# A gated-linear-attention layer with a routed expert layer on 8 cores: rows normalised earlier, four widths of tail products, rows loaded by a transposing DMA

## The reference

```
scores = (q * exp(A)) @ (k * exp(-A)).T, lower triangle       # A = cumsum(log f) in the chunk
o      = scores @ v + (q * exp(A)) @ S
S      = exp(A_last) * S + (k * exp(A_last - A)).T @ v        # k = 1 - exp(log f)
```

## Time and profile before

| | |
|---|---|
| median of three runs | 2378.13 us |
| profiled execution: its time / span of the slowest core (core 4) | 2381.81 us / 2380.2 us |
| spans of the eight cores | 2348.0 to 2380.2 us |
| TensorE matmuls busy | 2251.3 us (95%) |
| VectorE / ScalarE / POOL busy | 1066.1 (45%) / 700.0 (29%) / 331.9 us (14%) |
| TensorE's mean granted clock, core 4 | 0.979 |
| chain that ended last: TensorE / DMA / VectorE | 71% / 14% / 8% |
| HBM read and written | 577.84 MB and 109.05 MB |

### The profile page before, as it was taken

The page is one execution under the profiler, slowest core; times in us unless marked ns, Lnnn a source line. Parts: engine busy times, 40 slices in busy tenths (PEclk is TensorE's granted clock), DMA queues, the critical chain, the costliest instruction groups (busy, mean ns, idle before and its releaser), DMA issues.

```text
span 2380.2 us, 44339 instructions; the slowest of 8 cores (2348.0 to 2380.2 us)
## 1 busy us (share of the span) xinstructions
PE 2251.3 (95%) x15680; PEld 1401.6 (59%) x15680; DVE 1066.1 (45%) x2174; ACT 700.0 (29%) x1346; POOL 331.9 (14%) x539
## 2 busy tenths in 40 slices
PE   5999998989998999999999999999999999998997
PEld 4666554556645655566444457767666586683443
DVE  6666665666655766565541231121121212211366
ACT  4444542355515553344321101121111212111000
POOL 1110110112101210111111011111101011011230
PEclk9999999999999999999999999999999999998998
DMA  7999976688838886698699689799999799999998
GB/s 124 198 191 220 197 136 162 184 160 151 148 137 186 158 139 131 185 205 139 131 259 222 153 243 180 160 191 191 242 193 194 149 186 202 185 222 185 245 317 286
DMA packets 110735, 445.55 MB, mean 187 GB/s; under 512 B 12416, under 2 KB 12432, under 8 KB 100368
## 3 DMA queue, kind: packets, MB, share of 16 engines
q0 software_dynamic: 76640, 278.47, 67.4%
q1 hardware_dynamic: 33840, 163.59, 19.6%
HBM read 577.84 MB, written 109.05 MB: 289 GB/s over the span
## 4 chain that ended last, share of the span: by engine, by line
PE 71%; DMA 14%; DVE 8%; issue 5%; ACT 1%; DVEq 0%; POOL 0%; SPq 0%; ACTq 0%; POOLq 0%
PE ps L773 14%; PE ps L732 12%; PE ps L448 11%; PE ps L742 9%; PE ps L461 8%; PE ps L422 6%; PE ps L433 6%; DMA wr<-w_t 3%; DVE FW L1120 3%; DMA out<-acc 2%; DMA eo<-eos 1%; PE ps L666 1%; DMA out<-y 1%; DVE Tt L1173 1%; DMA xp<-x_own 1%
## 5 line engine op out<-in xcount | busy, mean ns | idle before, releaser
L742 PE MATMUL ps<-xg,wr 128*128 128x256 bf16 (+2 forms) x2048 | 274.2, 287 | 5.0 <-issue 4.9
L773 PE MATMUL ps<-wr,gb 128*128 128x512 bf16 x1152 | 255.2, 384 | 7.4 <-DMA wr<-w_t 7.3
L433 PE MATMUL ps<-xT,wq 128*128 128x512 bf16 x1024 | 247.2, 385 | 8.6 <-ACT th L876 5.1
L1060 ACT ACTIVATE sil<-ps 128x256 bf16<-128x256 f32 (+2 forms) x160 | 74.8, 469 | 610.1 <-PE ps L732 477.9
L1603 POOL DMA_DIRECT2D wr<-w_t x240 | 128.1, 547 | 872.0 <-PE ps L742 385.7
L732 PE MATMUL ps<-xg,wr 128*128 128x256 bf16 x2048 | 244.7, 273 | 0.6 <-ACT eos L1080 0.4
L1445 DVE TENSOR_TENSOR gb<-sil,ps 128x256 bf16<-128x256 bf16 (+1 forms) x128 | 62.4, 488 | 407.5 <-PE ps L732 306.6
L448 PE MATMUL ps<-wv,xT 128*128 128x256 bf16 x2048 | 238.5, 276 | 5.2 <-DMA wv<-wv_t 2.1
L422 PE MATMUL ps<-xT,wk 128*128 128x512 bf16 x1024 | 233.7, 381 | 8.4 <-DMA wk<-wk_t 8.0
L461 PE MATMUL ps<-wo,ob 128*128 128x512 bf16 x1024 | 229.8, 383 | 6.4 <-DVE y L1295 3.7
L742 PEld LDWEIGHTS ps<-xg,wr 128*128 128x128 bf16 x2048 | 199.9, 98 | 55.3 <-issue 6.9
(11 more groups left out here) (159 smaller groups left out, 2559.6 us busy)
## 6 DMA issues: line engine op xcount, KB each, us to landing
wr<-w_t POOLq DMA_DIRECT2D x240, 512.0 KB, 29.5
wv<-wv_t POOLq DMA_DIRECT2D x64, 512.0 KB
wk<-wk_t POOLq DMA_DIRECT2D x64, 512.0 KB, 13.0
wq<-wq_t POOLq DMA_DIRECT2D x64, 512.0 KB, 12.0
xs<-x2T SPq DMA_DIRECT2D x40, 512.0 KB, 18.6
y1d<-y SPq DMA_DIRECT2D x20, 1024.0 KB, 5.5
xst<-xs SPq DMA_DIRECT2D x40, 512.0 KB, 19.1
eo<-eos SPq DMA_DIRECT2D x40, 512.0 KB, 9.2
```

What stands on the lines that cost most here:

```text
L433: ins = t.matmul(self.ps[:, b, :], self.wq[i % 2][:, k * 128:(k + 1) * 128], self.xT[q % 2][:, k, :], start=(k == 0), stop=(k == 15))
L742: ins = t.matmul(self.ps[:, bk, 0:w], self.wr[c % NRING][:, k * 128:(k + 1) * 128], self.xg[(b - 1) % 2][:, k, 256:256 + w], start=(k == 0 ...
L773: ins = t.matmul(self.ps[:, bk, :], lhs, self.wr[c % NRING][:, dg * 512:(dg + 1) * 512], start=(ic == 0), stop=(ic == 7))
L1060: a.activation(self.sil[n % 2][:, 0:w], self.ps[:, self.bank[0, b, ic, s], 0:w], AF.Silu).then_inc(self.a_sil, 1)
```

## The change

First, at steps h = 3, 6, 9, 12 of q = 2 and 3, ScalarE's Ln and Exp come right after the gates of the next step, and VectorE's norm comes after its gates and before its mask, both in the same step. TensorE's transposes stay in steps 4, 7, 10, 13. Second, the tail's width is one of four instead of three. Third, xst, its transposes and its copies go; SP loads xs by a DMA with transpose=True straight into xg. TensorE waits for the first two loads ahead of the first 256 slots and for the other three ahead of the tail. The loads of an expert wait for the hidden products that last read the buffer (block 0's for experts 0 and 1). The loads of s3x[1] for block 9 move from e == 6 to e == 5 and lose their wait.

```diff
-WIDTHS = (256, 304, CAP - 256)
+WIDTHS = (240, 272, 304, 384)
...
-            if b < NX:
-                self.pe_xg(t, b)
             self.pe_down(t, b)
...
-        if 0 < b < NB - 1:
-            t.wait_ge(self.a_xg, 5 * b)
-            t.wait_ge(self.v_xg, 5 * b)
...
+                    if 0 < b < NB - 1 and ic == 0 and wh == 0:
+                        for j in ((2, 3, 4) if s else (0, 1)):
+                            t.wait_ge(self.d_xg[j], 16 * b)
                     bk = self.take8(t, (wh, b, ic, s), (self.v_g, n) if wh else (self.a_sil, n))
                     if s and 0 < b < NB - 1:
-                        with t.If(self.count > 256 + WIDTHS[0]):
-                            with t.If(self.count > 256 + WIDTHS[1]):
+                        with t.If(self.count > 256 + WIDTHS[1]):
+                            with t.If(self.count > 256 + WIDTHS[2]):
+                                self.pe_tail(t, b, c, wh, bk, WIDTHS[3])
+                            with t.Else():
                                 self.pe_tail(t, b, c, wh, bk, WIDTHS[2])
+                        with t.Else():
+                            with t.If(self.count > 256 + WIDTHS[0]):
+                                self.pe_tail(t, b, c, wh, bk, WIDTHS[1])
                             with t.Else():
-                                self.pe_tail(t, b, c, wh, bk, WIDTHS[1])
-                        with t.Else():
-                            self.pe_tail(t, b, c, wh, bk, WIDTHS[0])
+                                self.pe_tail(t, b, c, wh, bk, WIDTHS[0])
...
+    def act_next(self, a, q, h):
+
+        if h in (3, 6, 9, 12) and 1 < q < 4:
+            self.act_rs1(a, ln_index(q + 1, h // 3 - 1))
...
             if g - 1 in VAT and g > 32:
                 self.act_gates(a, g + 1)
+                self.act_next(a, q, h)
                 self.act_ob(a, g - 1)
...
                 if g + 1 < NG:
                     self.act_gates(a, g + 1)
+                self.act_next(a, q, h)
                 if g > 31:
                     self.act_ob(a, g - 1)
...
-            if h in (3, 6, 9, 12) and 1 < q < 4:
-                self.act_rs1(a, ln_index(q + 1, h // 3 - 1))
...
-            if h in (4, 7, 10, 13) and 1 < q < 4:
-                self.dve_norm(v, ln_index(q + 1, (h - 4) // 3), self.xb)
...
             if g + 1 < NG:
                 self.dve_gates(v, g + 1)
+            if h in (3, 6, 9, 12) and 1 < q < 4:
+                self.dve_norm(v, ln_index(q + 1, h // 3 - 1), self.xb)
             self.dve_mask(v, g)
...
-    def sp_xst(self, s, e, j):
+    def sp_xg(self, s, e, j):
         if e == 0 and j == 0:
             for i in range(3):
                 s.wait_ge(self.d_sc[i], 32 * len(range(i, 16, 3)))
-            s.wait_ge(self.t_wo, 64)
-        if e:
-            s.wait_ge(self.t_xg, 5 * (e - 1) + j + 1)
+        if j == 0:
+            s.wait_ge(self.t_u3, HN[max(e - 1, 0), 7, 1])
         r = e * CAP + j * 128
-        s.dma_start(self.xst[j][:, :], self.xs[r:r + 128, :]).then_inc(self.d_xst[j], 16)
+        s.dma_start(self.xg[e % 2][:, :, j * 128:(j + 1) * 128], self.xs[r:r + 128, :],
+                    transpose=True).then_inc(self.d_xg[j], 16)
...
         self.sp_acc(s, 1)
-        for j in range(5):
-            self.sp_xst(s, 0, j)
         for a in range(2, 5):
             self.sp_acc(s, a)
+        for j in range(5):
+            self.sp_xg(s, 0, j)
         for a in range(8):
             self.sp_out(s, a)
             if a + 5 < 8:
                 self.sp_acc(s, a + 5)
             if a < 5:
-                self.sp_xst(s, 1, a)
+                self.sp_xg(s, 1, a)
...
-            if e == 6:
-                s.wait_ge(self.t_xg, 40)
+            if e == 5:
                 for tt in range(4):
                     s.dma_start(self.s3x[1][:, tt, :], self.x2d[12 + tt, :, :]).then_inc(self.d_s3x[1], 16)
```

More of the change, by code:

```diff
@@ L214, in __init__ @@
         self.xg = [at("xg%d" % i, [128, 16, CAP], BF16, 20480 * i) for i in range(2)]
-        self.xst = [at("xst%d" % i, [128, D], BF16, 40960 + 4096 * i) for i in range(5)]
         self.gb = at("gb", [128, 8, CAP], BF16, 77824)
@@ L263, in __init__ @@
         self.d_s3x = [sem("d_s3x%d" % i) for i in range(2)]
-        self.d_xst = [sem("d_xst%d" % i) for i in range(5)]
+        self.d_xg = [sem("d_xg%d" % i) for i in range(5)]
         self.d_eo = [sem("d_eo%d" % i) for i in range(2)]
@@ L328, in __init__ @@
         self.t_y = sem("t_y")
-        self.t_xg = sem("t_xg")
         self.a_sil = sem("a_sil")
         self.v_g = sem("v_g")
-        self.a_xg = sem("a_xg")
-        self.v_xg = sem("v_xg")
         self.a_eo = sem("a_eo")
@@ L656, in pe_program @@
             self.pe_general(t)
-    def pe_xg(self, t, e):
-        for j in range(5):
[L661 to L669, removed]
     def pe_ffn(self, t):
@@ L1065, in act_ffn @@
                     self.act_ex(a, 14 + ic)
-            if b < NX:
-                for j in range(5):
-                    n = 5 * b + j
-                    a.wait_ge(self.t_xg, n + 1)
-                    a.copy(self.xg[b % 2][:, 0:8, j * 128:(j + 1) * 128],
-                           self.pbf(self.bank["xg", n, 0]).rearrange("p (k t) -> p k t", t=128)
-                           ).then_inc(self.a_xg, 1)
             if 0 < b < NB - 1:
@@ L1456, in dve_ffn @@
                         self.dve_mix(v, T)
-            if b < NX:
-                for j in range(5):
-                    n = 5 * b + j
-                    v.wait_ge(self.t_xg, n + 1)
-                    v.tensor_copy(self.xg[b % 2][:, 8:16, j * 128:(j + 1) * 128],
-                                  self.pbf(self.bank["xg", n, 1]).rearrange("p (k t) -> p k t", t=128)
-                                  ).then_inc(self.v_xg, 1)
             if b == 0:
@@ L1809, in sp_program @@
                 for j in range(5):
-                    self.sp_xst(s, e + 1, j)
+                    self.sp_xg(s, e + 1, j)
             for tt in range(5):
```

## The result

Four runs of the changed kernel gave a median of 2470.45 us (2459.93 to 2472.13), four of the kernel before 2381.34 us on the same chip. The ratio is 1.0365, with a 95% interval of 1.0328 to 1.0402: **slower by 89 us**, where I had forecast 2384 us and a range up to 2440.

The account below looks back on a forecast made before the run. TensorE was taken to bound attention and experts with many rows, DMA those with few. Experts -5.8, norm +9.5, program +1 and SP +1 gave +5.7 us; against the median 2378.13 that meant 2384 us, range 2345 to 2440.

Parts of the forecast that it names:

- Program length: In the experts' tail products, the fourth copy lengthens TensorE's program: +1 us, bounds 0 and +5.
- The transposing loads: In the experts' stage, each row load takes 2.3 us of the DMA engines; the experts' net is -5.8 us.
- the recorded rival: In the experts' stage, loads take 3.5 us of the engines or more: median 2415 us, 2460 at 5 us; chance 0.28.
- Its sign: For costly loads in the experts' stage: POOL's weight-load bursts over 98 us apart in light experts, 94 being forecast.
- packet-price rival: In the experts' row loads, 2048 packets at 0.22 us each make 28 us a load: over 3000 us; chance 0.03.
- Queues: On SP, almost no slack at each expert's last load, hidden products covering the eo stores: +1 us, bounds 0 and +6.
- DMA or TensorE: In the experts' stage, DMA holds light experts at 90.5 us; TensorE bounds heavy ones, which gain 3.7 us each without transposes.
- The norm: In attention stages q = 2 and 3, new waits for sq and kT outweigh the removed xb waits: +9.5 us, bounds -20 and +14.
- works as meant: In attention stages q = 2 and 3, the norm's new waits hide, each stage gains: 2354 us; chance 0.15.
- The widths: In the experts' tail products, where TensorE sets the pace, core 4 gains 14 us and core 3 loses 1.8.

Follow-up runs that it names:

- run 3: The kernel before with four copies of the tail product at widths 256, 256, 304 and 384, so the same columns computed; 2448.73 us, ratio 1.0278.
- run 1: The kernel before with only the transposing loads of the change; 2441.94 us, ratio 1.0242.
- run 14: The kernel with the transposing loads alone, but untransposed, the same bytes put down in pieces of 256 B; 2414.43 us.
- run 13: The kernel with the transposing loads alone, but each a plain load of the same bytes in whole 4 KB rows; 2374.26 us, ratio 0.9981.
- run 7: The kernel with the transposing loads alone, but ScalarE issues the stores of eo and the loads wait for other hidden products; 2599.5 to 2646.7 us.
- run 15: The kernel with the transposing loads alone, but five buffers for eos instead of two; 2535.2, 2541.4 and 2551.8 us, ratio 1.0691.
- run 2: The kernel before with only Ln/Exp and the norm moved one head earlier; 2383.55 us, ratio 1.0005.
- run 9: The kernel before with the norm moved earlier, but Ln and Exp behind ob, sq, v and kT; slowest of cores 0 to 3 2370.8 us beside 2371.2.
- run 4: The kernel before with only the four widths 240, 272, 304 and 384; 2447.94 us, ratio 1.0263.
- run 10: The kernel before with its three copies, but widths 272, 304 and 384; slowest of cores 0 to 3 2371.4 us beside 2371.2.
- run 5: The kernel before with the four widths, the width chosen once per expert in four long branches; 2454.2 and 2454.9 us.
- run 11: The kernel with the transposing loads alone, but two of five loads issued between the previous expert's stores; slowest of cores 0 to 3 2475.6 us.

## Why the prediction was wrong, point by point

**Program length: the step that failed.** I wrote "The fourth copy lengthens TensorE's program; today 4.9 us on core 4 are spent waiting for nothing visible in front of tail products. I take +1, bounds 0 and +5." It measured +67 us by itself (run 3), which alone leads past my upper bound of 2440. The row was read, and taken as the price of a jump to be scaled up. It was the first sign of a limit on how fast code arrives, one packet in some 6.9 us, at which the kernel stood already with its three copies. The upper bound was worked out from a slope, and no row of before excludes a step.

**The transposing loads, the second term that failed.** I took 2.3 us of the engines, 0.7 above the plain 1.6. Run 1's +61 us stands against a term that was to bring a gain of 5.8 us in the experts. It lies in the recorded rival, "A load takes 3.5 us of the engines or more", for which I had 2415 us at 3.5 and 2460 at 5; 2441.94 lies between, at some 4.4 us. By q1's share it is 4.1, by all queues together 2.6, so that the rival's size is right as a price in time and not shown as one of the engines alone. Its sign is right too: in run 1 the bursts for light experts with loads beside them are 102.0, 94.6 and 104.6 us apart on core 4. My choice of the nearest row (the plain load of the same bytes) was the mistake: the packets went up by 77440, 1936 a load, as the "pieces of 256 B" of my upper bound had them. But the price a packet of the earlier trace rows, 0.22 us, was taken from packets of 4.8 KB. Run 14 shows at most 1.0 us for 1920 more packets over 16 engines, 8 ns each. The packet-price rival of over 3000 us is excluded by it.

The Trainium skill (Advanced Engine Details and Errata, X-Bar Transpose (TRN2)) says that such loads are as fast as regular ones. Runs 1 and 13, which differ in the load alone, disagree: 2441.94 against 2374.26 us. In a quieter stretch of run 1 (1341.89 to 1365.62 us on core 0, DMA share 0.85) SP issued five in 23.73 us, 4.7 us each.

**Queues.** "The stores of eo behind the loads have 60 us of hidden products as cover." SP was held 90 to 102 us for five loads, so the cover was too short; I had counted the loads' engine time and no time of issue. That wait is real (82.2 us in run 1), but without it the slowest core takes longer (runs 7 and 15), so it isn't what sets the time there.

**DMA or TensorE.** That DMA holds the light experts was right: without the 80 transposes an expert (run 13) the gain is 7 us, not 30. On core 4 the bursts of three light experts are 88.5, 89.5 and 95.3 us apart there, 90.4, 91.2 and 90.5 before, while the first heavy expert goes from 100.1 to 97.5, 2.6 us where I had 3.7: the wait ahead of the down product, which I took as 0.9 us, is 1.8 in the changed kernel. At the plain price and without new widths my terms give core 4 four heavy experts at -3.7 and +1 for SP, -13.8 us, and core 3 three of them, -10.1. Their medians went from 2377.0 to 2364.8 (-12.2) and from 2365.6 to 2344.9 (-20.7). The agreement on core 4 is partly luck: core 0, with four heavy experts too, gained 4.4 us and core 5 19.6, so the terms don't tell the cores apart.

**The norm.** Waits for sq were forecast as 1.1, 2.5 and 3.8 us at h = 3, 6 and 12, and for kT as 2.8 us at h = 9, in each of two stages, 20.4 in all. Measured are none, 2.5 and 3.4, and 2.0 in the first stage, none, 2.2 and 3.4, and 2.8 in the second, 16.3 in all. The waits on xb went, as forecast. So the places and nearly all sizes are right. The term was +9.5, and measured are +2.3 at block 0 and no difference at the end, neither clear of scatter. The waits came out 4.1 us smaller. The slow stretch of 1.6 us that I charged behind each of six stalls is there behind four, at a granted clock of 0.50 to 0.73: after the 3.4 us before 606.20 the granted clock is 0.50 and 32 value products take 6.13 us, where after the 2.2 us before 800.77 it is 1.00 and they take 3.65. Where the rest of the 9.5 went isn't settled. The norm's rival "works as meant" is false in both orders (runs 2 and 9).

**The widths** save columns as counted, and nothing shows of it (runs 4 and 10).

**The sum.** 67 + 61 + 2 = 130, and the measured loss is 89. The causes overlap: the waits for eos fall from 82.2 us (run 1) to 18.5, and the program's waits stay. That TensorE, held up by the issue waits, asks for weights more slowly and so leaves room for the loads fits this and wasn't tested.

## What to carry to other kernels

The bodies of a short branch are paid for in instruction traffic whether they run or not; long bodies are in part left out, and then the jump waits. Where a profile shows a few microseconds of "issue" in front of short products, with the DMA engines full, read it as a limit that may have been reached, not as a small price, and count how much code a microsecond of work needs. A transfer is priced by its bytes, its packets, its kind and the hold on its issuing queue, so swap the same bytes in as plain rows to see what the kind of transfer costs. And a wait that goes away may have been the brake that kept a fuller resource working: three edits aimed at the largest wait of run 1 made the slowest core slower by 48 us and more. No version here beats the kernel before but the one with plain rows, by 7 us, and that one leaves the transposition out.

## What the runs showed of the hardware that was not expected

- Issue waits of the hidden products on core 0 go 0, 10.7, 67.8 us for 153, 170 and 187 instruction packets. With four copies the packets (16.4 KB, about 1 us each) start 6.9 us apart in the median, where the products would need one in 5.3 to 5.8 us by the estimate above.
- Bodies of 32 instructions that are skipped are fetched in full; of bodies of 1024 instructions about two thirds are not (169 packets in run 5).
- A jump over a whole expert's code waits up to 11.5 us with plain traffic beside it, and up to 22.4 us with transposing loads.
- Behind an issue wait of 3.68 us the granted clock was 0.50, and two groups took 6.5 us instead of 3.7.
- Five loads of 2048 packets hold the issuing queue for 87 us beside POOL's weight loads, transposed or not, where plain rows take 3.65 us. In a quieter stretch five transposing loads took 23.7 us.
- In run 15 the engines show a share of 1.25 at 134 GB/s. In the execution whose trace was kept three other cores took 4301 to 11854 us, at a granted clock of 0.55 to 1.0; core 7, whose rows stand above, took 2536.4 us in it, near its 2539.8 in another execution and far from its 2359.8 and 2359.6 in two more. Why is open. In run 11 one execution took 2996 us, at a granted clock down to 0.74.
